# A three-layer conditioned block on one core: gated weights, gate rows, single-tile turns and the order at the start of attention

## What is computed

```python
def _bitlinear(x, w, nw, b=None):
    xn = x * rsqrt(mean(square(x), -1) + 1e-08) * nw
    y = _act_quant(xn) @ _weight_quant(w).T      # weights: round(w / mean|w|) clipped to -1..1
...
h = _bitlinear(silu(c), wa0, na0)
h = _hgrn_mlp(h, wa1, na1, wa2, na2)
h = _rmsnorm(_bitlinear(h, wa3, na3, ba3), wr, 1e-06)
s_msa, sc_msa, g_msa, s_mlp, sc_mlp, g_mlp = split(_bitlinear(h, wa4, na4, ba4), 6)
mx = _layernorm(x) * (1 + sc_msa) + s_msa
i = _bitlinear(mx, wi, ni); f = sigmoid(_bitlinear(mx, wf, nf)); g = _bitlinear(mx, wg, ng)
o = _hgrn_scan(silu(i) * (1 - f), f)             # h[t] = f[t] h[t-1] + i[t]
x = x + g_msa * _bitlinear(_rmsnorm(o, gn, 1e-05) * silu(g), wo, no_)
x = x + g_mlp * _hgrn_mlp(_layernorm(x) * (1 + sc_mlp) + s_mlp, wm1, nm1, wm2, nm2)
```

## Time and profile before

| | us |
|---|---|
| median of 3 runs | 465.76 (465.52 to 466.42) |
| the profiled execution | 466.24 |
| its span in the profile | 464.4 |
| TensorE busy in the span | 322.8 |
| VectorE busy | 292.2 |
| ScalarE busy | 258.0 |
| GpSimd busy | 118.8 |

### The profile page before, as it was taken

The page is one execution under the profiler, slowest core; times in us unless marked ns, Lnnn a source line. Parts: engine busy times, 40 slices in busy tenths (PEclk is TensorE's granted clock), DMA queues, the critical chain, the costliest instruction groups (busy, mean ns, idle before and its releaser), DMA issues.

```text
span 464.4 us, 6129 instructions
## 1 busy us (share of the span) xinstructions
PE 322.8 (70%) x2108; PEld 152.3 (33%) x2108; DVE 292.2 (63%) x678; ACT 258.0 (56%) x564; POOL 118.8 (26%) x178
## 2 busy tenths in 40 slices
PE   0239964452245736599989998877777889998786
PEld 0127543321114512122222234644422233333264
DVE  2677587657667668998888633255577566663130
ACT  2667777364465411578888885343405555666542
POOL 0011019940363542010000010323301232322410
PEclk9999999999965767599999999999865899998799
DMA  7950170000000052200000000000432000000001
GB/s 253 416 218 1 47 320 3 1 0 1 1 0 0 0 137 68 68 2 1 3 2 1 3 2 1 1 1 0 112 93 68 2 1 4 2 2 1 2 0 47
DMA packets 11941, 21.89 MB, mean 47 GB/s; under 512 B 2043, under 2 KB 10623, under 8 KB 11263
## 3 DMA queue, kind: packets, MB, share of 16 engines
q1 hardware_dynamic: 11908, 21.49, 13.5%
HBM read 14.54 MB, written 0.52 MB: 32 GB/s over the span
## 4 chain that ended last, share of the span: by engine, by line
PE 43%; DVE 23%; ACT 15%; POOL 8%; issue 7%; SPq 2%; DMA 1%; DVEq 0%; ACTq 0%; POOLq 0%
PE pe L1595 9%; ACT big L1253 7%; DVE nm L967 7%; PE pe L1617 7%; PE pe L1649 5%; PE pe L1570 4%; PE pe L1495 3%; PE pe L1573 3%; POOL rstd L358 3%; PE pe L1545 2%; DVE xn L529 2%; PE pe L1460 2%; DVE st L519 2%; PE pe L1360 1%; SPq L328 1%
## 5 line engine op out<-in xcount | busy, mean ns | idle before, releaser
L967 DVE TENSOR_REDUCE nm<-pe 128x2 f32<-128x1024 f32 (+2 forms) x112 | 124.3, 1145 | 41.6 <-PE pe L1573 30.2
L1253 ACT ACTIVATE big<-pe 128x512 f32<-128x512 f32 (+3 forms) x256 | 116.3, 522 | 51.0 <-PE pe L1617 48.5
L1595 PE MATMUL pe<-big,scr 128*32 128x256 f32 (+3 forms) x704 | 65.8, 451 | 3.2 <-ACT scr L1226 2.9
L1570 PE MATMUL pe<-big 62*128 62x512 bf16 (+3 forms) x256 | 51.8, 380 | 18.4 <-DVE nm L967 17.0
L1617 PE MATMUL pe<-big 64*128 64x512 bf16 (+3 forms) x256 | 58.0, 365 | 8.1 <-DVE scr L858 4.8
L358 POOL TENSOR_TENSOR rstd<-var,half 128x4 f32<-128x4 f32 x26 | 28.0, 1078 | 115.1 <-DVE var L524 76.0
L1617 PEld LDWEIGHTS pe<-big 64*128 64x128 bf16 x256 | 16.4, 94 | 65.7 <-ACT big L1253 36.0
L441 POOL CAST nm<-nm 128x16 bf16<-128x16 f32 x16 | 3.1, 196 | 122.0 <-DVE nm L967 122.0
L451 POOL TENSOR_SCALAR_AFFINE_SELECT big<-big 128x512 f32<-128x512 f32 x32 | 20.1, 635 | 31.4 <-ACT big L1253 30.9
L529 DVE TENSOR_SCALAR xn<-x_tok,mv,rstd 128x128 f32<-128x128 f32 x64 | 18.5, 353 | 14.1 <-POOL rstd L358 13.9
L1205 ACT ACTIVATE hT<-pe,modc 128x512 f32<-128x512 f32 x12 | 9.3, 778 | 32.2 <-PE pe L1360 32.2
(11 more groups left out here) (196 smaller groups left out, 577.7 us busy)
## 6 DMA issues: line engine op xcount, KB each, us to landing
big<-tern SPq DMA_DIRECT2D x48, 128.0 KB, 2.4
big<-in_fill SPq DMA_DIRECT2D x1, 4096.0 KB, 12.7
big<-in_wa SPq DMA_DIRECT2D x1, 2304.0 KB, 12.4
w<-in_w SPq DMA_DIRECT2D x2, 1152.0 KB, 18.5
big<-in_w SPq DMA_DIRECT2D x1, 1024.0 KB, 14.2
w<-in_w SPq DMA_DIRECT2D x1, 896.0 KB, 20.3
rowg<-in_rowg SPq DMA_DIRECT2D x1, 832.0 KB, 18.2
big<-in_wa SPq DMA_DIRECT2D x1, 704.0 KB, 6.1
```

Source lines behind the costliest of these rows:

```text
L967: v.tensor_reduce(dst, src[:, :, 0:w * len(pairs)].rearrange("p r (h w) -> p r h w", w=w), AX.X, ALU.max, negate=True).then_inc(sem(f"a{a} ...
L1253: s_.activation(P[:, kt % PRING, 2 * p + j, q0:S], bank[SINGLES[i % 3]][:, q0:S], ACT.Exp, scale=SCALE).then_inc(sem(f"a{a}_p"), 1)
L1570: last = t_.matmul(dsts[par][:, k * wd:(k + 1) * wd], QZ[rows, b, 2 * g + i, qt * 128:(qt + 1) * 128], KZ[rows, b, 2 * g + i, 0:wd], start ...
L1595: last = t_.matmul(bank[PV_BANK][32 * h:32 * h + 32, lo:hi], V[b][:, kt, HG * g + h, :], P[:, k % PRING, h, lo:hi], start=(kt == 0), stop= ...
```

## The change

- The six magnitude sums of `w0` stand ahead of the fourth total, which now covers all the remaining matrices; the fifth total, its scales and its wait are gone.
- `gate_rows` has no bias rows. `gate_rows(0)` goes behind the last product of the condition, the other two behind the second scan's turn and the broadcast of the remaining parameters. They use banks 3 and 7, and ScalarE copies them later (`gates(1)`, `gates(2)` ahead of `quantise(1, ...)`). GpSimd adds the bias rows to the gates (`whole_gates`).
- GpSimd's gated weights leave their place ahead of the scan's gate. The first step comes after the last root before layer 0's MLP, the other five and the masked biases come inside the first attention, after the parts of the maxima of units 0 to 5 (`APART`). Each product waits for its own step only.
- `turn` and the turns in the attention wait tile by tile. `normed` and `quantise` signal each tile.
- In the first attention, batch 1's turn comes after the first maximum (`"x"` in `START`) and q, k, v each one maximum later.
- Of the 12 stacking copies of batch 0, ScalarE now issues 4 (`lower_pieces`: k's middle pieces, both low pieces), SP 8.

```diff
@@ -206,7 +206,7 @@
-TOTALS = (7, 6, 1, 7, 5)
+TOTALS = (7, 6, 1, 7)
@@ -224,9 +224,9 @@
-START = {8: {1: ("q",), 2: ("k",), 3: ("v",), 9: ("q_high",), 10: ("k_high",), 12: ("low",)},
+START = {8: {1: ("x",), 2: ("q",), 3: ("k",), 4: ("v",), 9: ("q_high",), 10: ("k_high",), 12: ("low",)},
...
-OUTSIDE = ("q", "k", "v", "q_high", "k_high", "low", "norm")
+OUTSIDE = ("x", "q", "k", "v", "q_high", "k_high", "low", "norm")
@@ -328,8 +328,10 @@
-        for part in range(3):
-            stack(0, part)
+        stack(0, 0)
+        sp.wait_ge(sem(f"a{a}_mid"), 1)
+        for j in [j for j, piece in enumerate(PIECES) if piece == 1]:
+            sp.dma_start(QZ[j::SLOT, 0, :, :], spl[:, 0, 1, 0, :]).then_inc(sem(f"a{a}_stack0"), 16)
@@ -371,11 +373,17 @@
-    pool.wait_ge(sem("ld_w123"), 16 * 5)
-    pool.wait_ge(sem("gates"), 3)
-    for n, (w, at, k, layer, which) in enumerate((
-            (w1, ATT_W["proj"], 1, 0, 0), (w1, ATT_W["fc2"], 4, 0, 1), (w2, L2_W["w2"], 2, 1, 0),
-            (w2, L2_W["f2"], 2, 1, 1), (w3, ATT_W["proj"], 1, 2, 0), (w3, ATT_W["fc2"], 4, 2, 1))):
+    mask_bias = row0[:, 0:B * TB * D].rearrange("p (t d) -> p t d", d=D)
...
+    def whole_gates(l):
+        pool.wait_ge(sem("gates"), l + 1)
+        g = gbc[:, l].rearrange("p b k d -> p b (k d)")
+        link(nc.gpsimd.tensor_tensor(g, g, wide(rowg[:, 2 * D * l:2 * D * (l + 1)], B), ALU.add))
...
+    def gated_weights(n):
...
+        w, at = WG0[n]
+        k, layer, which = (1, 4, 2, 2, 1, 4)[n], n // 2, n % 2
@@ -385,6 +393,16 @@
+        pool.wait_ge(sem("wg"), n + 1)
...
+    def masked_biases(b):
+        for t in tiles(b):
+            link(nc.gpsimd.tensor_scalar(mask_bias[:, t], gate_bias(2, b), maskf[:, t:t + 1], None, ALU.mult))
...
+    APART = {0: lambda: (whole_gates(1), whole_gates(2)), 1: lambda: gated_weights(1), 2: lambda: gated_weights(2),
+             3: lambda: (gated_weights(3), masked_biases(0)), 4: lambda: (gated_weights(4), masked_biases(1)),
+             5: lambda: gated_weights(5)}
@@ -396,6 +414,9 @@
+    pool.wait_ge(sem("ld_w123"), 16 * 5)
+    whole_gates(0)
+    gated_weights(0)
@@ -453,6 +469,8 @@
+                    if item == "parts" and n == 0 and u in APART:
+                        APART[u]()
@@ -523,11 +541,13 @@
-    def normed(b, wait, count):
+    def normed(b, wait, count, each=None):
...
+            if each:
+                last.then_inc(sem(each), 1)
@@ -627,11 +647,7 @@
     def wide_scales():
-        weight_scales(4, 4, 5)
-        dve.sem_inc(sem("wscales"), 1)
...
-    def main_scales():
-        weight_scales(5, 5, 11)
+        weight_scales(4, 4, 11)
@@ -1059,7 +1074,7 @@
     def gates(l):
-        s_.copy(gbc[:, l].rearrange("p b k d -> p (b k d)"), bank[(1, 4, 5)[l]]).then_inc(sem("gates"), 1)
+        s_.copy(gbc[:, l].rearrange("p b k d -> p (b k d)"), bank[(1, 3, 7)[l]]).then_inc(sem("gates"), 1)
@@ -1077,7 +1092,11 @@
-    wide_magnitudes(1).then_inc(sem("absum"), 1)
+    wide_magnitudes(1)
+    act.wait_ge(sem("ld_w0"), 16)
+    for j in range(6):
+        last = magnitudes(5 + j, w0_f[:, W0_AT[j]:], NWA + W0_AT[j], W0_N[j])
+    last.then_inc(sem("absum"), 1)
@@ -1087,12 +1106,6 @@
-    act.wait_ge(sem("ld_w0"), 16)
-    for j in range(6):
-        last = magnitudes(5 + j, w0_f[:, W0_AT[j]:], NWA + W0_AT[j], W0_N[j])
-    last.then_inc(sem("absum"), 1)
-    gates(0)
-    act.wait_ge(sem("wscales"), 2)
@@ -1115,8 +1128,8 @@
-            last = s_.activation(dst[:, t], src[:, t], ACT.Identity, bias=magic[:, 0:1], scale=q4[:, 3, m, t:t + 1])
-        last.then_inc(sem(done), 1)
+            s_.activation(dst[:, t], src[:, t], ACT.Identity, bias=magic[:, 0:1],
+                          scale=q4[:, 3, m, t:t + 1]).then_inc(sem(done), 1)
     def mx_squares(b):
@@ -1137,8 +1150,7 @@
         if b == 0:
-            gates(1)
-            gates(2)
+            gates(0)
@@ -1163,6 +1175,8 @@
+    gates(1)
+    gates(2)
@@ -1208,8 +1222,24 @@
+            def lower_pieces():
...
+                if a == 0:
+                    act.wait_ge(sem("zeroed"), 16)
+                act.wait_ge(sem(f"a{a}_mid"), 2)
+                for j in [j for j, piece in enumerate(PIECES_K) if piece == 1]:
+                    s_.dma_start(KZ[j::SLOT, 0, :, :], spl[:, 1, 1, 0, :]).then_inc(sem(f"a{a}_stack0"), 16)
+                for qk, (dst, pieces) in enumerate(((QZ, PIECES), (KZ, PIECES_K))):
+                    act.wait_ge(sem(f"a{a}_split"), qk + 1)
+                    j = pieces.index(2)
+                    s_.dma_start(dst[j::SLOT, 0, :, :], spl[:, qk, 2, 0, :]).then_inc(sem(f"a{a}_stack0"), 16)
...
+                if b == 1 and a == 0:
+                    lower_pieces()
...
+                if b == 1 and a == 1:
+                    lower_pieces()
@@ -1316,22 +1346,18 @@
     def gate_rows(l, w):
-        out_ = bank[(1, 4, 5)[l]]
+        out_ = bank[(1, 3, 7)[l]]
...
-            t_.matmul(out_[:, 2 * b * D:2 * (b + 1) * D], ones[0:1, :], rowg[0:1, 2 * D * l:2 * D * (l + 1)],
-                      start=True, stop=False)
...
-                                 w[:, part * D:(part + 1) * D], start=False, stop=(k == 1))
+                                 w[:, part * D:(part + 1) * D], start=True, stop=True)
...
-    pe.wait_ge(sem("absum"), 4)
-    t_.matmul(bank[7][:, 11:12], ones[:], absum[:, 11:12], start=True, stop=True)
-    weight_totals(4, 4, 5)
+    weight_totals(4, 4, 12)
@@ -1339,24 +1365,22 @@
-    gate_rows(0, w1)
...
-    weight_totals(5, 5, 11)
...
-    gate_rows(1, w2)
-    pe.wait_ge(sem("wscales"), 2)
-    gate_rows(2, w3)
...
-    def turn(bk, src, b, done=None):
+    gate_rows(0, w1)
...
+    def turn(bk, src, b, done=None, made=None, at=None):
...
+            if made:
+                pe.wait_ge(sem(made), TB * (b if at is None else at) + i + 1)
@@ -1372,14 +1396,10 @@
-        if b:
-            pe.wait_ge(sem("gates"), 3)
...
-            pe.wait_ge(sem("qm_a"), 3 * b + m + 1)
-            turn(4 * b + 2 * m, vq[m], b, "qm_aT")
-        pe.wait_ge(sem("qm_a"), 3 * b + 3)
+            turn(4 * b + 2 * m, vq[m], b, "qm_aT", "qm_a", 3 * b + m)
...
-        turn(4 * b, vq[2], b, "qm_aT")
+        turn(4 * b, vq[2], b, "qm_aT", "qm_a", 3 * b + 2)
@@ -1398,9 +1418,11 @@
+    for l, w in ((1, w2), (2, w3)):
+        pe.wait_ge(sem("ss_o"), l)
+        gate_rows(l, w)
...
-        pe.wait_ge(sem("qm_o"), b + 1)
-        turn(4 * b, vq[1], b, "qm_oT")
+        turn(4 * b, vq[1], b, "qm_oT", "qm_o")
@@ -1433,20 +1455,18 @@
-    pe.wait_ge(sem("qm_b"), 1)
-    turn(2, xn, 0, "qm_bT")
+    pe.wait_ge(sem("gates"), 3)
+    turn(2, xn, 0, "qm_bT", "qm_b")
...
-    pe.wait_ge(sem("qm_b"), 2)
-    turn(6, xn, 1, "qm_bT")
+    turn(6, xn, 1, "qm_bT", "qm_b")
...
     def attention_turn(n, b):
-        pe.wait_ge(sem("n_xn"), B * n + b + 1)
-        turn(TURN_BANK, xn, b, "n_T")
+        turn(TURN_BANK, xn, b, "n_T", "n_xn", B * n + b)
     def attention_products(n, b, which=(0, 1)):
@@ -1502,8 +1522,8 @@
-            attention_turn(n, 1)
...
+                attention_turn(n, 1)
@@ -1521,6 +1541,8 @@
             def ring_item(item, u, i=0):
+                    if item == "x":
+                        attention_turn(n, u)
```

22 lines of the change are left out of this document (8 added, 14 removed).

## The result

The changed kernel takes 454.22 us (median of four executions, 454.17 to 454.94) against 466.09 for the kernel before beside it: a ratio of 0.9748, 95% interval 0.973 to 0.9766. The profiled execution took 454.17 with a span of 452.4, so 12.1 less than the profiled one of before. Medians leave out two executions at a lower clock, one of 530.14 us of the run with both edits undone and one of 486.88 us of the kernel before.

What follows compares the result with a forecast made beforehand. The prediction took a chain of waits, hopping between engines from 20 to 170 us, as the bound; -10.5 - 0.35 + 0.4 - 1.2 - 0.95 - 1.0 = -13.6 from 466.24 gave 452.6, by the median 452.2; range 449.3 to 457.3.

Steps and rivals of the forecast that it cites:

- Step 1: Condition: totals together and gate rows out of the way bring the first multiply 2.7 us earlier, the first squares 6.1.
- Step 2: Gated scan: gates out of it, no GpSimd wait, unstretched VectorE operations and single tiles make it 12.3 us earlier in all.
- Step 3: Behind the second scan: two sets of gate rows ahead of the turn give back 1.8 us, net -10.5.
- rival C: More than counted: gate rows slide under the table load, factors lose nothing, turns save 0.8 each; 449.2 us, chance 0.13.
- Step 4: GpSimd beside VectorE: -0.35 us net after the stage's last root, +0.4 for a low part meeting bias sums in the attention.
- Step 5: Attention starts: split copies land earlier and batch 1's turn is spread over maxima; -1.2 us in the first, -0.95 in the second.
- Rival A: Attention starts: one generator serves both queues, so copies go out in turn and land no earlier; 455.2 us, chance 0.14.
- Step 6: MLPs: turns tile by tile after a norm, about two of them on the chain, save 1.0 us.
- D: Slower: the new start leaves TensorE at its lower clock in the first attention; near 480 us, chance 0.03.
- the rows named as signs: If right: first squares near 50, gated scan near 78.5 without GpSimd wait, turn waiting for gate rows, maximum before batch 1's turn.
- the 94.7: Sign of being right: TensorE's turn after the second scan waits for its own gate rows, near 94.7 us.
- the wrong signs: `ld_w0` wait near 26, first maximum released by a copy at 171 minus the shift, stretched reductions, clock under 1.00.

Runs made afterwards that it cites:

- run with both edits undone: The changed kernel with SyncE issuing every stacking copy and batch 1's turn ahead of the first maximum again; 454.29 us, ratio 0.9731.
- the run with two of them: The kernel before with totals together and the gated weights moved; gate rows, gate copies and turns as before; 459.88 us, ratio 0.9871.

## Why the prediction came out as it did

**Step 1** (-6.1 at the squares, measured -6.2) was right in size and mixed in cause. Totals together give 4.6; the other 1.6 comes from the first set of gate rows, and its copy, out of the way: where they stay, ScalarE waits 3.10 for them. The step counted their leaving only for the turn at 44.27. It also did not see that 6 us at the squares would run into the rows of layers 2 and 3: the earlier trace rows shows the first set only, and the others end at 61.1 in the kernel before, no wait behind them. The sum held because the change halves and moves them as well.

**Step 2** (-12.3, measured -12.5): right, term by term: no wait for GpSimd, line 747 unstretched, one gate copy less. The single tiles were put at 0.7 and measured 0.74. The terms are not additive, as the run with two of them showed (6.2 for 4.1 and 5.2).

**Step 3** (+1.8, measured +0.24) failed in its size. The mechanism was right, since the turn does stand behind its gate rows; the size was not. 4.6 us for two sets was scaled from the earlier trace rows, at the lower level. They ran at 3.75, the turn behind them at 0.61 in place of 1.12, the product behind it at 0.40 in place of the 0.61 seen without them, and the table load covers the rest. That was half of rival C.

**Step 4**: between the residual and the first copy 0.9 was won, where 0.35 was forecast. The single tiles give all of it (0.9 in the run without them). The loss beside GpSimd came, a factor of 1.15 in place of 0.16, but by the next multiply of that stage it was gone, so it was not on the chain, and the 1.4 put against it was too much. In the attention the conflict with the sums came at the instruction named, 1.15 in place of 0.67, 0.48 for the 0.4. The Trainium skill (SBUF — State Buffer, Who interferes with whom) has this as an exclusive lock for VectorE operations with two SBUF inputs; the run with the sums moved agrees, 1.14 to 0.67.

**Step 5** (-1.2 and -0.95) failed, and it is the largest miss. The first maximum's product came 0.55 nearer to the first copy, batch 1's q product 1.04 further, the score product 1.29 further; in the second attention the first maximum's product came 0.16 nearer. Two things were wrong. The landing was taken as 2.4 behind an issue on either queue: it is 3.3 to 4.0 by line when both issue, and data comes 0.25 earlier, not 1 to 2. And the turn behind the maximum was taken as harmless for VectorE's sake, where TensorE at its lower level is busy without a gap and pays 0.56 for it. The 1.29 is not all this step's. 0.48 is the conflict of step 4, and 0.89 is the level, at the values (1.83 against 1.16) and the pair ahead of them (0.61 against 0.39), so order and copies together come to nothing where -1.2 was forecast. Rival A gives the same outcome, no gain from the copies, but not by its cause: the issues of the two queues did not go out in turn. The Trainium skill (DMA: Bandwidth & Descriptors, Issuing engines are not separate DMA queues) says that issuing from several engines saves only the sequencer's time for it; the trace agrees (5.4 us of issuing instead of 7.8), and the rows with the landings show what the prediction took from it too readily, that the saved time is not yet an earlier landing. Its rule of an exclusive generator (Perfetto Trace Analysis, DMA Instruction — HWDGE) no run here decides: issues on both queues last 0.61, but the row does not show the generator.

**Step 6** (-1.0): right. 0.3 at each of two turns and 0.2 at a third by the run without single tiles.

**The sum** forecast 1.5 more gain than the profiled executions show, and that it is so near is partly luck, since misses of both signs cancel. Up to the residual the forecast gain was 1.7 too small, nearly all in step 3, and up to the first copy another 0.5. From the first copy to the maxima's row one unit on it was 2.9 too large: 1.2 of step 5, and 1.6 of the level, which no step held (0.89 above and 0.73 at a product set of line 1617, 1.93 against 1.20). Behind that it was 0.95 too large, 0.8 of it the second half of step 5. **D** did not happen: from 189 to 273 the granted clock is 1.00. But the level it speaks of is what blurs every difference under 2 us here. Of the rows named as signs, the first squares, the gated scan and the first maximum ahead of the turn came as said. The turn stands behind its gate rows, but at 91.56: the 94.7 took the net -10.5, with step 3's delay in it, off a time that already held that delay. VectorE's reductions were not stretched (1145 ns on average in both traces). One of the wrong signs came, the first maximum released by a copy at 157.61, which is 170.7 on the old clock.

## What to carry to other kernels

A wait that shows in a trace is only the longest of those that end at that place: before counting a gain of 6 us, look in each queue for what has no wait now but ends within those 6 us of being needed. A distance between two rows compares two kernels only if TensorE ran at the same level between them. A duration of TensorE taken from one stretch holds for another only if its level does; cost such a term at both levels and keep both in the range. Splitting copies over two issuing queues gains when issuing is the limit, so look first at how busy the DMA engines are while one queue issues: at 0.75 of their time the split won 0.25 us here.

## What the runs showed of the hardware

Copies of 128 KB issued from two queues at once landed 2.7 to 4.5 us behind their issue (the changed kernel's lines 334, 1231 and 1235), against 2.3 to 2.6 from one, with the DMA engines' busy share above 1 instead of 0.75. TensorE's level held at 1.00 through the first attention's start when it had products during its 7 us wait, and a product of 128x512 in f32 took 1.12 instead of 2.08; in the second attention four such products, issued when the level had already begun to fall, brought it back for 8 us and delayed the first maximum by 2.5. Executions of one kernel differed by up to 5.7 us. A product of a gate row, 128x128 in f32, took 0.25 to 0.29 us at the higher level and 0.61 at the lower. A VectorE multiply of 128x512 with two SBUF inputs took 0.67 alone and 1.15 beside one of GpSimd's sums.
